# Attention rounds with scores and masks ahead of the next chunk's transposes, and a state term in four matmuls

## The reference, cut to what matters

```python
q = (x @ W_q.T).reshape(b, t, h, dh)      # k, v alike
decay = jnp.where(diff >= 0, gammas[:, None, None] ** pow_, 0.0)
attn = jnp.einsum('bihd,bjhd->bhij', q, k) * decay[None] / scale
y = jnp.einsum('bhij,bjhd->bihd', attn, v)
```

## Time and profile before

| | |
|---|---|
| median of 3 runs | 962.76 us (961.16 to 964.6) |
| profiled execution, its own time | 965.13 us |
| its span in the trace | 963.1 us |
| mean granted TensorE clock | 0.955 |
| PE, DVE, ACT, POOL busy | 89%, 79%, 60%, 58% of the span |

### The profile page before, as it was taken

One profiled execution on the slowest core, in us unless ns is written; L12 is line 12 of the kernel. 1 busy time (PEld: TensorE's weight loads), 2 busy tenths in 40 slices (PEclk: granted clock), 3 DMA queues, 4 the chain that ended last, 5 costly groups with the idle time before them and its releaser, 6 DMA issues.

```text
span 963.1 us, 22162 instructions
## 1 busy us (share of the span) xinstructions
PE 857.8 (89%) x7040; PEld 805.8 (84%) x7040; DVE 763.6 (79%) x1156; ACT 573.5 (60%) x1009; POOL 561.7 (58%) x409
## 2 busy tenths in 40 slices
PE   3949889889888888799899999999999999999865
PEld 1438778778777777699899999999999999999855
DVE  5687877777777778847888888888888888888476
ACT  3824444444443444338677787777777777777541
POOL 2217565666666666535566666666666666666254
PEclk9959999999999999959999999999999999999877
DMA  9923333333333333355577677777677777777487
GB/s 304 354 86 97 92 86 85 80 80 82 85 81 84 85 80 82 85 226 175 191 239 226 227 235 232 227 229 231 228 231 229 230 229 229 229 229 221 140 263 254
DMA packets 106249, 170.49 MB, mean 177 GB/s; under 512 B 30768, under 2 KB 77232, under 8 KB 96240
## 3 DMA queue, kind: packets, MB, share of 16 engines
q1 hardware_dynamic: 99408, 151.49, 51.4%
q0 software_dynamic: 6816, 18.69, 5.2%
HBM read 115.88 MB, written 33.18 MB: 155 GB/s over the span
## 4 chain that ended last, share of the span: by engine, by line
PE 60%; DVE 21%; issue 8%; ACT 3%; DMA 3%; another core or an unknown queue 2%; DVEq 1%; POOL 1%; SPq 0%; ACTq 0%
PE ps L706 23%; PE ps L904 22%; DVE arena_r L1142 5%; PE ps L794 5%; DVE arena_f L1149 4%; PE ps L779 2%; PE ps L889 2%; DMA arena_f<-pair_rows 2%; PE ps L819 1%; PE ps L724 1%; PE ps L762 1%; DVE arena_f L1173 1%; DVE y_stats L1165 1%; ACT arena_r L567 1%
## 5 line engine op out<-in xcount | busy, mean ns | idle before, releaser
L706 PE MATMUL ps<-arena_r 128*128 128x256 f32 (+1 forms) x2256 | 291.7, 285 | 20.1 <-DVE arena_f L1173 18.0
L706 PEld LDWEIGHTS ps<-arena_r 128*128 128x128 f32 x2256 | 277.6, 193 | 26.3 <-issue 24.2
L486 POOL TENSOR_TENSOR arena_r<-arena_f,arena_r 128x2048 fp32r<-128x2048 f32 x39 | 191.5, 4909 | 134.3 <-ACT arena_r L560 134.3
L904 PE MATMUL ps<-arena_r 128*128 128x256 f32 x1872 | 234.0, 285 | 0.8 <-DVE gn_t L1298 0.8
L904 PEld LDWEIGHTS ps<-arena_r 128*128 128x128 f32 x1872 | 230.3, 194 | 0.9 <-issue 0.9
L1235 DVE TENSOR_SCALAR arena_f<-arena_f 128x256 f32<-128x256 f32 x78 | 156.0, 2040 | 1.4
L560 ACT ACTIVATE arena_r<-arena_f 128x2048 fp32r<-128x2048 f32 x78 | 145.5, 1919 | 1.6 <-PE ps L706 1.6
L467 POOL TENSOR_TENSOR arena_r<-arena_f,arena_r 128x512 fp32r<-128x512 f32 x64 | 93.7, 1475 | 57.4 <-ACT arena_r L567 55.7
L819 PE MATMUL ps<-arena_r 128*128 128x128 f32 x1024 | 126.1, 284 | 0.0
L819 PEld LDWEIGHTS ps<-arena_r 128*128 128x128 f32 x1024 | 123.5, 201 | 0.0
L639 ACT ACTIVATE arena_f<-ps,arena_f 128x256 f32<-128x256 f32 x156 | 65.0, 471 | 94.3 <-PE ps L904 73.2
(11 more groups left out here) (141 smaller groups left out, 1060.2 us busy)
## 6 DMA issues: line engine op xcount, KB each, us to landing
arena_f<-w SPq DMA_DIRECT2D x78, 1024.0 KB, 6.0
xs_rows<-spare_rows SPq DMA_DIRECT2D x39, 258.0 KB, 3.3
arena_f<-xs_rows SPq DMA_DIRECT2D x39, 258.0 KB, 2.9
arena_r<-arena_r SPq DMA_DIRECT2D x256, 32.0 KB
pair_chunk<-xn SPq DMA_DIRECT2D x32, 256.0 KB, 2.6
arena_f<-pair_rows SPq DMA_DIRECT2D x16, 512.0 KB, 5.4
arena_f<-b SPq DMA_DIRECT2D x39, 128.0 KB, 4.5
xn<-x SPq DMA_DIRECT2D x8, 512.0 KB, 8.8
```

Source lines behind the costliest of these rows:

```text
L486: nc.gpsimd.tensor_tensor(w1_r[par][:, 1], w1_raw[par], w1_r[par][:, 0].bitcast(F32), ALU.subtract).then_inc(s["w1_l"], 1)
L706: last = pe.matmul(out_ap, lhs(a), rhs(b), start=start and n == 0, stop=stop and n == 2, **kw)
L904: last = pe.matmul(ps[:, 2 + hp, o * SLOT:(o + 1) * SLOT], w1_r[par][:, a, at:at + P], xs_r[:, b, k * SLOT:(k + 1) * SLOT], start=(m == 0 ...
```

## The change

PE computes the scores of chunk i first in its round, and transposes keys and queries of i+1 behind them. ACT copies the high parts of score groups 0 and 1 ahead of the high part of those transposes. DVE does its four masks ahead of the low part of the transposes. The state term `across` sends the high and low part of the state as one operand of 256 columns against the high part of the queries, and the high part of the state against the low part of the queries: four matmuls a round in place of six. `projections` and `new_state` are each cut into two functions that are called one after the other; that moves nothing. Mask groups 1 and 3 get a wait on the low parts of the round before, which DVE itself has made.

```diff
--- before.py
+++ after.py
@@ -568,14 +568,14 @@
 
             def chunk(i, par):
                 n, np_ = i + 1, 1 - par
-                if within(n, NT):
-                    act.wait_ge(s["kqt_psum"], n + 1)
-
-                    wait(act, s["across_done"], n - 1)
-                    nc.scalar.activation(kq_t[:, np_, :, 0], ps[:, 5, :].rearrange("p (w n) -> p w n", w=2), ACT.Copy).then_inc(s["kqt_h"], 1)
                 if within(i, NT):
                     score_high(i, par, 0)
                     score_high(i, par, 1)
+                if within(n, NT):
+                    act.wait_ge(s["kqt_psum"], n + 1)
+
+                    wait(act, s["across_done"], n - 1)
+                    nc.scalar.activation(kq_t[:, np_, :, 0], ps[:, 5, :].rearrange("p (w n) -> p w n", w=2), ACT.Copy).then_inc(s["kqt_h"], 1)
                 if within(i + 2, NT):
                     m = i + 2
                     act.wait_ge(s["xt_psum"], m + 1)
@@ -753,7 +753,7 @@
                     last = pe.transpose(ps[:, 4, k * P:(k + 1) * P], x_chunk[par][:, k * P:(k + 1) * P], ident)
                 last.then_inc(s["xt_psum"], 1)
 
-            def projections(n, par):
+            def key_value_projection(n, par):
 
                 pe.wait_ge(s["xt_h"], n + 1)
                 pe.wait_ge(s["xt_l"], n + 1)
@@ -762,6 +762,8 @@
                         last = pe.matmul(ps[:, 4, :], xt[:, par, a, k * P:(k + 1) * P], wkv[:, b, k, :],
                                          start=(m == 0 and k == 0), stop=(m == 2 and k == KC - 1))
                 last.then_inc(s["kv_psum"], 1)
+
+            def query_projection(n, par):
 
                 wait(pe, s["kqt_h"], n)
                 wait(pe, s["kqt_l"], n)
@@ -804,8 +806,11 @@
                 wait(pe, s["y_f"], n)
                 y_bank = ps[:, 7, :].rearrange("p (h s d) -> p h s d", h=H, s=2)
                 for c in range(KC):
-                    last = parts(y_bank[:, c * HP:(c + 1) * HP, 0], lambda a: kq_t[:, par, 1, a, c * P:(c + 1) * P],
-                                 lambda b: state_r[:, b, c * P:(c + 1) * P], c == 0, False, skip_group_check=True)
+                    heads = y_bank[:, c * HP:(c + 1) * HP]
+                    both = state_r[:, :, c * P:(c + 1) * P].rearrange("p s (h d) -> p h s d", h=HP)
+                    pe.matmul(heads, kq_t[:, par, 1, 0, c * P:(c + 1) * P], both, start=(c == 0), stop=False, skip_group_check=True)
+                    last = pe.matmul(heads[:, :, 0], kq_t[:, par, 1, 1, c * P:(c + 1) * P], state_r[:, 0, c * P:(c + 1) * P],
+                                     start=False, stop=False, skip_group_check=True)
                 last.then_inc(s["across_done"], 1)
 
             def inside(n, par):
@@ -844,10 +849,10 @@
                 last.then_inc(s["yt_psum"], 1)
 
             def chunk(i, par):
+                if within(i, NT):
+                    scores(i, par)
                 if within(i + 1, NT):
                     kq_transposes(i + 1, 1 - par)
-                if within(i, NT):
-                    scores(i, par)
                 if within(i + 2, NT):
                     x_transposes(i + 2, par)
                 if within(i - 1, NT):
@@ -856,7 +861,8 @@
                 if within(i - 2, NT):
                     y_transposes(i - 2, par)
                 if within(i + 2, NT):
-                    projections(i + 2, par)
+                    key_value_projection(i + 2, par)
+                    query_projection(i + 2, par)
                 if within(i, NT):
                     across(i, par)
 
@@ -865,7 +871,8 @@
             x_transposes(0, 0)
             pe.wait_ge(s["w_split_h"], 3)
             pe.wait_ge(s["w_split_l"], 3)
-            projections(0, 0)
+            key_value_projection(0, 0)
+            query_projection(0, 0)
 
             pe.wait_ge(s["route_mask"], 1)
             pe.wait_ge(s["tables_done"], 3)
@@ -1144,15 +1151,17 @@
             def masked_scores(i, g):
                 dve.wait_ge(s["s_psum"], NB * i + g + 1)
 
-                if g % 2 == 0:
-                    wait(dve, s["s_l_pool"], 2 * (i - 1) + g // 2 + 1 if not isinstance(i, int) or i > 0 else 0)
+                low = s["s_l_pool"] if g % 2 == 0 else s["s_l_dve"]
+                wait(dve, low, 2 * (i - 1) + g // 2 + 1 if not isinstance(i, int) or i > 0 else 0)
                 V.tensor_tensor(s_f[:, g].rearrange("p (h i) -> p h i", h=HB), ps[:, g, :].rearrange("p (h i) -> p h i", h=HB),
                                 C["causal"].unsqueeze(1).to_broadcast([P, HB, P]), ALU.mult).then_inc(s["s_f"], 1)
 
-            def new_state(m):
+            def state_sum(m):
                 dve.wait_ge(s["u_psum"], m + 1)
                 dve.wait_ge(s["st_f"], m + 1)
                 V.tensor_tensor(state_t, ps[:, 6, 256:512].rearrange("p (c i) -> p c i", c=KC), state_f, ALU.add).then_inc(s["st_t"], 1)
+
+            def new_state(m):
                 dve.wait_ge(s["st_t"], m + 1)
 
                 wait(dve, s["st_h"], m)
@@ -1174,16 +1183,17 @@
                                 ps[:, 7, :].rearrange("p (h s d) -> p h d s", h=H, s=2), AX, ALU.add).then_inc(s["y_f"], 1)
 
             def chunk(i, par):
-                if within(i + 1, NT):
-                    transposed_low(i + 1, 1 - par)
                 if within(i, NT):
                     for g in range(NB):
                         masked_scores(i, g)
+                if within(i + 1, NT):
+                    transposed_low(i + 1, 1 - par)
                 if within(i + 2, NT):
                     tokens_low(i + 2, par)
                 if within(i, NT):
                     score_low(i, par, 1)
                 if within(i - 1, NT):
+                    state_sum(i - 1)
                     new_state(i - 1)
                 if within(i, NT):
                     score_low(i, par, 3)
```

6 lines of the change are left out of this document (3 added, 3 removed).

## The result

The changed kernel takes 994.32 us (median of 4 runs, 993.57 to 996.88) against 963.68 us (961.16 to 964.84) for the kernel before, a ratio of 1.033 with a 95% interval of [1.030, 1.036]. The forecast was 973.0 with a range of 961 to 996: slower, as said, but by 30.6 us instead of 10. The profiled execution took 994.72 us, its span is 992.7 us.

The account below looks back on a forecast made before the run. The prediction took a closed loop through SP's diagonal DMAs (11.17 us a round) or a stalled round (11.69) as the bound; middle 11.43 against 11.10, +0.33 over 31 rounds, +10.3 us, gave 973.0, range 961 to 996.

Parts of the forecast that it names:

- TensorE's low clock: Rival, chance 0.18: PE idle ahead of the output transposes drops to 1.2 GHz in half the rounds; P 12.0, 991 us.
- The loop through the diagonal: Mask, copies, subtraction, SP's eight diagonal DMAs, landing, scores, next mask form one closed loop: 11.17 us a round, ends 10.70 and 11.97.
- the late mask: Rival, chance 0.12: scores to mask stays 2.24 us, not the scatter's doing; loop 12.26 us, 999 us.
- Scores to mask: Step from PE's scores to DVE's first mask: 1.15 us, between 0.98 and 1.35, once no scatter runs beside the scores.
- The scatter moves to 12.8 - P: POOL's scatter starts 12.8 - P after the first mask, P being the round length: 1.6 us at 11.17.
- DVE first means 11.17, POOL first means 11.69, and each keeps itself up: Race of DVE's low part (3.5 us after the mask) against POOL's (3.9 or 3.4) sets the round length, either outcome self-sustaining.
- the stalled round: Round in which POOL's low parts hold DVE's low part and delay the state term: 23.4 - P, so 11.69 us.
- the early round: Profiled round of the kernel before, its DVE low part taking 2.73 us, ending 6.04 after the scatter's start; used as model.
- the 2.90 us row: Profile row of the kernel before: key and value projection took 2.90 us instead of 1.62 at granted clock 0.50.
- the saving is worth nothing in the 11.17 loop: State term in four matmuls saves about 0.28 us, but PE then waits for the diagonal, so no gain there.
- the row used in the prediction: Profile row with DVE's low part held over 2 us by both POOL instructions, preferred to the skill's rule of one.

Follow-up runs that it names:

- order_only: The changed kernel with the state term put back to six matmuls, so the new order alone: 1017.54 us, 1.049 against the kernel before.
- after_filler: The changed kernel with 14 matmuls that nothing reads ahead of PE's output transposes: 973.60 us, 1.011 against the kernel before.
- state_four: The kernel before with the state term in four matmuls and nothing else: 960.02 us, 0.994 against the kernel before.
- after_between_loads: The changed kernel with VectorE's low part between the masks, ACT's transposes copy first and scatter loads ahead of the diagonal DMAs, no filler: 940.51 us.

## Why the prediction was right in sign and short by two thirds

The step that failed is the sum itself: it puts TensorE's low clock at nothing and keeps it as a rival. With the clock back at 1.00 the 31 rounds take 354.1 us, with it at 0.87 they take 377.7: 23.6 us of the 34.6. Point by point:

- **The loop through the diagonal: right.** Predicted 3.37 + 4.55 + 2.0 + 0.1 + 1.15 = 11.17 us; the short rounds take 11.06 to 11.47. From mask to SP's first DMA 3.25 us (213.32 to 216.57), the landing 2.0, the waits for the DMA ahead of the scores as described. Taking it away at full clock is worth 1.3 us a round. The forecast put it at next to nothing (11.17 against 11.10), since the late mask had lengthened the old round, which is 10.05 without it.
- **Scores to mask: right in size, its cause open.** 1.1 us in the rounds whose scores take 0.98 (224.98 to 226.09), 1.35 in those whose scores take 1.3 (211.97 to 213.32), the granted clock 1.00 in both. The rival of the late mask is out for the changed kernel, but it came back in order_only, and a scatter beside the scores isn't enough to cause it.
- **The scatter moves to 12.8 - P: right.** Its first issue starts 1.35 us after the mask (214.67) behind a round of 11.33 us, and 0.34 ahead of it (225.75) behind one of 12.77; the formula gives 1.47 and 0.03.
- **"DVE first means 11.17, POOL first means 11.69, and each keeps itself up": wrong in both halves.** VectorE's low part came first by the rows, 3.41 us after the mask (216.73; 3.5 in the sum), POOL's pair at 216.95, and VectorE was held all the same, so who comes first didn't decide. And P in the formula is that of the round before, so a long round pulls the next scatter ahead of the mask, and the rounds alternate. That alone would have been harmless: at full clock the stalled round is 11.4 us, not 11.69, because the low part ends 5.4 us after the scatter's start and not the 6.04 of the early round (after_filler), and the total at full clock is 973.6. The forecast of 973.0 is, by its own sum, that of a kernel whose clock stays at 2.4 GHz. That the two agree within 1 us is partly luck: the forecast took the middle between two kinds of round, 11.43, and the runs have one kind, stalled, at 11.4.
- **The clock: the term that was left out.** It stood as a rival with 0.18, at P = 12.0 and 991 us, against it only that "the clock is 0.99 over the stretch now". Measured 12.06 to 12.18 and 994: the rival was right in place (projections 2.80 us behind the idle time ahead of the output transposes, in about half of the rounds). Its price came out by two errors that cancel: it put 11.69 us for the stalled round and 0.3 for the clock, the runs have 11.4 and 0.76 (23.6 us over 31 rounds). The forecast itself had PE wait for the diagonal in each round, and longer for the state sum in the stalled one, and the clock of a stretch without those waits said little about one with them. The prediction did name "a granted clock under 0.9 in the attention" as what would prove it wrong; it was 0.87. The sum should have charged the 2.90 us row to every stalled round. By the medians of after_filler the clock holds about 20 of the 30.6 us.
- **"Either way … the saving is worth nothing in the 11.17 loop": wrong as to the changed kernel.** The saving in time is small, as said (first matmul of the state term to the scores 0.51 us, 224.47 to 224.98, against 0.71 for the six matmuls of the state sums, 226.52 to 227.23: 0.20 where 0.28 was taken), but six in the new order cost 16 to 23 us, with a lower clock and late masks beside it.
- **The Trainium skill**, SBUF — State Buffer, "Who interferes with whom", has the shared port locked for a whole instruction, by which VectorE should get in after one of GpSimd's. Here its low part (216.73) ended at 220.04, 0.59 us after the second of POOL's pair (216.95 to 219.45): it was held by both, as the row used in the prediction had it, though its own record starts first. That one waits for the other is borne out, the single instruction isn't.

That PE's idle time is what lowers the clock is shown in both directions: filling 1.87 us of it raised the clock to 1.00, and shortening both waits without any filler (0.6 us a round ahead of the output transposes, 0.2 to 0.3 ahead of the scores) raised it to 0.98. Which idle time does it isn't settled: the kernel before holds 0.99 with waits of 0.8 us and 0.65 us a round (19.0 us and 15.5 us over 24 rounds), and after a wait of 1.4 us the clock falls in one round and not in the next. So is why the parts outside the 31 rounds are 5.0 us shorter in the changed kernel and 6 us in state_four; I had set the gains and losses there against each other.

## What to carry to other kernels

When a reorder puts a wait of 1.4 to 2.2 us into TensorE's round, price the work behind the wait at 1.2 GHz too before anything else, and write a self-reinforcing loop as a sequence of rounds rather than as one fixed point. Two experiments separate the causes quickly: matmuls that nothing reads in the idle time, put where they can't lie on the chain, and the stall removed; neither alone tells, since the one hid the other here. Look also at what shares a queue: three loads ahead of eight DMAs were worth 21 us in the old order.

## What the runs showed of the hardware

- The order of DMAs in SP's queue set when VectorE's mask could start, though the mask doesn't wait for the loads that were moved: 2.24 us from scores to mask with the three loads behind the eight diagonal DMAs, 1.34 with them ahead, and 963 to 942 us in all. In the kernel before, the late masks start 1.6 to 1.7 us behind the second POOL indirect DMA; in after_between_loads such a DMA beside the 24 matmuls delays nothing (1.34 us).
- 14 matmuls a round that compute nothing made the kernel 20.7 us faster (994.3 to 973.6 us), with the granted clock at 1.00 instead of 0.87.
- A VectorE subtraction of 0.68 us took 3.31 us beside two POOL subtractions that follow each other (2.50 us together), and ended 0.59 us behind the second.
- Six matmuls of 128 columns start 0.12 us apart (0.71 us for six). In the state term of four, the two of 256 columns take 0.12 and 0.16 us to the next start and the two of 128 columns 0.07 and 0.16 (224.47, 224.59, 224.66, 224.82, scores at 224.98): the number of matmuls sets the price here, not the columns.
